# Moving weighted values in TensorE's order of an attention kernel, so that a pair of maxima comes right behind each

## The reference

```
q, k = rope(q), rope(k)
scores = where(causal, q @ k.T / sqrt(16), -inf)
y = softmax(scores) @ v + gating * softmax(q @ ak.T / sqrt(512)) @ av
x = layernorm(x + y @ w_proj.T)
base = x @ base_w.T + base_b;  hidden = x @ A.T;  probs = softmax(x @ router_w.T)
combine = top 2 of probs, divided by their sum
x = layernorm(x + base + 0.5 * sum_e combine[e] * (hidden @ B[e].T))
```

## Time and profile before

| | us |
|---|---|
| median of 3 runs (lowest to highest) | 1001.28 (1001.17 to 1004.49) |
| the profiled execution's own time | 1001.27 |
| its span, first to last instruction | 999.6 |
| PE busy in the span | 900.8 |
| DVE busy | 743.1 |
| ACT busy | 490.0 |
| POOL busy | 240.8 |

### The profile page before, as it was taken

How to read it: one execution, slowest core, us unless ns; L and a number is a source line. 1 busy time by engine, 2 the same in 40 slices (tenths; PEclk the granted TensorE clock), 3 DMA queues, 4 the chain that set the end, 5 groups by cost and what they waited for, 6 DMA issues and landing times. The chain is left out here.

```text
span 999.6 us, 16360 instructions
## 1 busy us (share of the span) xinstructions
PE 900.8 (90%) x5420; PEld 502.0 (50%) x5420; DVE 743.1 (74%) x2254; ACT 490.0 (49%) x1027; POOL 240.8 (24%) x252
## 2 busy tenths in 40 slices
PE   2899999948899999999999999999848999999996
PEld 1778787841222222222223222322237888888884
DVE  3475746569898988889898889896156677777765
ACT  3243334340477777777777777777831211221210
POOL 0215252433121222222222222222202122122211
PEclk9999999985699999999999999999968999999998
DMA  6124242425543335554334545336110010110100
GB/s 216 35 72 116 65 114 74 115 82 128 96 94 58 65 74 96 96 96 81 62 63 84 97 97 96 70 63 158 48 43 11 22 42 21 42 42 21 43 32 31
DMA packets 50401, 74.05 MB, mean 74 GB/s; under 512 B 8864, under 2 KB 21408, under 8 KB 50208
## 3 DMA queue, kind: packets, MB, share of 16 engines
q1 hardware_dynamic: 50336, 73.24, 31.5%
HBM read 56.17 MB, written 16.78 MB: 73 GB/s over the span
## 5 line engine op out<-in xcount | busy, mean ns | idle before, releaser
L720 ACT ACTIVATE pt<-bank 128x512 f32<-128x512 f32 (+3 forms) x768 | 335.2, 493 | 133.2 <-PE bank L1229 122.5
L896 DVE CUSTOM_DVE_ANT_0 bank<-bank,cmask 128x512 f32<-128x512 f32 (+3 forms) x512 | 234.5, 525 | 15.9 <-PE bank L1239 14.1
L1229 PE MATMUL bank<-qs,ks 98*128 98x512 bf16 (+3 forms) x768 | 209.7, 335 | 23.6 <-ACT pt L720 23.3
L578 POOL TENSOR_SCALAR_AFFINE_SELECT pt<-pt 128x512 f32<-128x512 f32 x128 | 81.2, 635 | 368.7 <-ACT pt L720 368.7
L1272 PE MATMUL bank<-pt,vb 128*32 128x512 f32 (+3 forms) x1536 | 164.5, 500 | 0.9 <-POOL pt L578 0.9
L899 DVE TENSOR_REDUCE mx<-bank 128x1 f32<-128x512 f32 x256 | 159.0, 685 | 4.7 <-PE bank L1239 2.6
L1239 PE MATMUL bank<-km,qm 48*128 48x512 bf16 (+3 forms) x768 | 138.9, 347 | 15.7 <-DMA km<-k_parts 11.7
L1229 PEld LDWEIGHTS bank<-qs,ks 98*128 98x128 bf16 x768 | 59.7, 96 | 160.1 <-ACT pt L720 98.2
L1239 PEld LDWEIGHTS bank<-km,qm 48*128 48x128 bf16 x768 | 34.9, 95 | 145.4 <-DVE mx L896 64.0
L745 ACT CAST xth<-bank 128x512 fp32r<-128x512 f32 x16 | 9.4, 585 | 153.8 <-PE bank L1334 153.8
L896 DVE DVE_READ_ACCUMULATOR2_ANT mx<- 128x1 f32 x512 | 73.4, 143 | 0.0
(11 more groups left out here) (141 smaller groups left out, 1378.5 us busy)
## 6 DMA issues: line engine op xcount, KB each, us to landing
qs<-q_parts SPq DMA_DIRECT2D x32, 256.0 KB, 4.7
q_parts<-part SPq DMA_DIRECT2D x48, 128.0 KB, 2.4
k_parts<-part SPq DMA_DIRECT2D x48, 128.0 KB, 2.4
ks<-k_parts SPq DMA_DIRECT2D x16, 384.0 KB, 6.9
xs<-in_xT SPq DMA_DIRECT2D x10, 512.0 KB, 3.6
qm<-q_parts SPq DMA_DIRECT2D x32, 128.0 KB, 7.8
km<-k_parts SPq DMA_DIRECT2D x32, 128.0 KB, 7.3
qs<-q_parts SPq DMA_DIRECT2D x32, 128.0 KB, 3.3
```

Source lines behind the costliest of these rows:

```text
L578: gp.affine_select(out=blk, in_=blk, compare_op=ALU.is_ge, fill=0.0, base=0, pattern=[[0, HG], [1, P]], channel_multiplier=-1).then_inc(S( ...
L720: act.activation(pt[k % PT_BUFS][:, h, 0:width(st)], half(n % SCORE_BUFS)[:, 0:width(st)], ACT.Exp, scale=float(HD) ** -0.5).then_inc(S("e ...
L896: last = ve.tensor_tensor_reduce(blk, blk, cmask[:, BANK - nk * P:], 1.0, NEG, ALU.add, ALU.max, mx[m][:, 0, h, qt:qt + 1])
L1229: pe.matmul(half(n % SCORE_BUFS)[:, 0:q1 - q0], ks[g % 2][0:KX, h, kb * P:(kb + 1) * P], qs[g % 2][0:KX, h, q0:q1], start=True, stop=True) ...
```

## The change

The places of the weighted values are found together with those of the slots: a place must be a score that has two or more slots right behind it, ahead of the next score, and each step takes the first such place at or after the one of `value_place`. As the transposes' places depend on those of the last steps, the two are worked out in turn, five times.

```diff
-VALUES_AT = [value_place(st) for st in range(NS)]
...
+def place_values(first):
+
+    follow = [c for c in range(SCORE_BANKS) if first[(c + 1) % SCORE_BANKS + 1] - first[(c + 1) % SCORE_BANKS] >= 2]
+    at = []
+    for st in range(NS):
+        n = max(value_place(st), at[-1] + 1 if at else 0)
+        if st == LAST_STEP[0] + 1:
+            n = max(n, at[-1] + SCORE_BUFS)
+        while n % SCORE_BANKS not in follow:
+            n += 1
+        at.append(n)
+    while at[-1] - SCORE_BANKS + SCORE_BUFS > at[0]:
+        at[0] += 1
+        while at[0] not in follow:
+            at[0] += 1
+    return at
+
+
+NORM_CHUNK = [9, 25]
+for _ in range(5):
+    VALUES_AT = place_values(place_slots(NORM_CHUNK)[0])
+    COPY_AT = [VALUES_AT[st] for st in LAST_STEP]
+    NORM_CHUNK = [COPY_AT[1] - SCORE_BANKS + 5, COPY_AT[0] + 5]
...
+FIRST, NORM_AT, ROWS_AT = place_slots(NORM_CHUNK)
```

More of the change, by code:

```diff
@@ L100, in value_place, with place_slots @@
     return n
-VALUES_AT = [value_place(st) for st in range(NS)]
[L104 to L108, removed]
 SLOTS = NMX + 3
-NORM_CHUNK = [COPY_AT[1] - SCORE_BANKS + 5, COPY_AT[0] + 5]
 NORM_OF = [(-1, 1), (0, 0)]
-def place_slots():
+def place_slots(norm_chunk):
     read = [sum(nk * P + READ_START for _, _, nk in max_of((LEAD + n) % NMX)[2]) for n in range(NMX)]
@@ L126, in place_slots @@
         first.append(slot)
-        if c in NORM_CHUNK:
+        if c in norm_chunk:
             norm_at.append(slot)
@@ L137, in place_slots @@
     return first + [SLOTS], norm_at, rows_at
-FIRST, NORM_AT, ROWS_AT = place_slots()
+def place_values(first):
[18 more added lines that the diff above has]
+    NORM_CHUNK = [COPY_AT[1] - SCORE_BANKS + 5, COPY_AT[0] + 5]
+assert VALUES_AT == sorted(set(VALUES_AT)) and COPY_AT[0] < SCORE_BANKS <= COPY_AT[1]
+FIRST, NORM_AT, ROWS_AT = place_slots(NORM_CHUNK)
 CALC_AT = ROWS_AT - ROWS_LAG
```

## The result

Over 20 executions each, the changed kernel takes 1006.85 us in the median (1002.39 to 1010.39) and the kernel before 1002.27 (1000.77 to 1007.65); the ratio is 1.0037 with a 95% interval of 1.0019 to 1.0055. So the change makes the kernel slower by about 0.4%, inside the 0.5% that was called no change. Against the range of 993 to 1006.5: the 1001.28 us that the forecast starts from, times the ratio, is 1005.0, inside, while the median of the 20 by itself lies 0.35 above its upper end. The profiled execution took 1002.41 us, 1.14 more than the profiled one of before. The median moved by 4.6. Both numbers need an explanation. One execution of the kernel before, beside e1 to e4, took 1055.56 us at a mean clock of 0.825 and is in no comparison.

What follows compares the result with a forecast made beforehand. TensorE's order of work, with its switches and waits on ScalarE, was taken to bound attention; span 999.6 - 1.0 + 0.5 + 1.4 = 1000.5, plus 1.7 gives 1002.2 us, range 993 to 1006.5.

Steps and rivals of the forecast that it cites:

- Switches: TensorE in each attention head group: six changes of kind fewer at 0.095 us, saving 0.57 us a group.
- Waits that take their place: TensorE's scores waiting on ScalarE: 2.37 us instead of 1.86, +0.51 a group; period 29.32, -1.0 us over 14 groups.
- The last group: Attention's last head group, without maxima and bound by ScalarE: no switch saved, between 0 and +1, taken as +0.5 us.
- The first group: Attention's first head group, partly at half clock: full clock rises later behind a later first block; 0 to +3, taken +1.4 us.
- so no correction: Starting time: the profiled run's 1001.27 us taken as typical, since the three runs' median is 1001.28.
- A: Attention groups: saved switches arrive whole and ScalarE's waits do not grow, -0.57 x 14 = -8.0, 993.8 us; chance 0.15.
- B: Attention groups: the copy's stall returns whole, 0.82 at scores 11 and 27, +1.40 a group, 1022.8 us; chance 0.08.
- C: Attention groups: both stalls shrink and nothing replaces them, -2.04 a group to 27.35, about 973 us; chance 0.06.

Runs made afterwards that it cites:

- e1: The changed kernel once more, unaltered, beside the kernel before: 1004.79 us, ratio 1.0019.
- e4: A third order of weighted values, pairs of maxima and transposes, written out, against the kernel before: 965.57 us, ratio 0.9632, period 26.74 us.
- e2: Half of the change: only four blocks of weighted values that end no half moved, against the kernel before: 1005.97 us, ratio 1.0050, period 29.48 us.
- e3: The other half: only blocks that end a half moved, with ScalarE's copies and transposes, against the kernel before: 1003.67 us, ratio 1.0019, period 29.41 us.
- e7: The kernel before with added products that keep TensorE at work ahead of group 0, against the kernel before: 1001.44 us, ratio 0.9984.
- e8: The changed kernel with the same added products ahead of group 0 as e7, against the kernel before: 1001.67 us, ratio 0.9982.
- e6: The kernel before with two pairs of maxima moved into the two stalls behind ScalarE's copies: 992.15 us, ratio 0.9889, period 28.63 us.
- e5: The kernel before with pairs of maxima moved to the blocks; blocks, copies and transposes stay: 981.53 us, ratio 0.9777, period 27.95 us.
- e9: The order of e4 with the added products ahead of group 0, against the kernel before: 967.61 us, ratio 0.9658, period 26.74 us.
- e10: Another written-out order of values, pairs and transposes, with the added products, against the kernel before: 972.06 us, ratio 0.9701, period 27.15 us.

## Why the prediction was right, and where not

**Switches.** Right: 6 x 0.095 = 0.57. In the profile after, a block holds TensorE 1.00 us ahead of a pair as ahead of a score, and the count fell by six, from 55 to 49. The Trainium skill, TensorEngine Tiling (Array Packing), Key Properties, says that changing the tiling mode drains TensorE, while another tile of the same mode does not; the rows agree: scores and transposes, both on the whole array, follow each other at no cost, and a change from scores to pairs, from pairs to scores or from scores to strips of 32 columns costs 0.09 to 0.10. What leaving the strips costs can't be read apart, as nothing but a change ever follows a block.

**Waits that take their place.** Right to 0.04 us: 19.20 was walked for the stretch from the pair of 0 to that of 33, 19.24 measured, with the late starts at the scores named (6, 23, 32) and in the sizes given (0.42, 0.47, 0.37 for 0.42, 0.46, 0.38). VectorE's idle time of 1.22 before the first normalisation is gone, and the one ahead of the pair of score 9, foreseen as 0.8, is 0.76:

```profile
500.05 0.70 DVE L916 CUSTOM_DVE_ANT_0 bank<-bank,cmask 128x512 f32<-128x512 f32 x1 [0.76 <-PE bank L1259]
```

The period came out at 29.35 for 29.32; over 14 groups -0.55 for -1.0.

**The last group.** +0.73 for +0.5, inside its bounds. ScalarE idles 1.02 and 0.65 us ahead of the two copies there, against 0.37 and none before, more than the 0.3 more that was walked.

**The first group.** +1.35 for +1.4 in the profiled execution, but the reason given did not hold. The term was built on the rise following the first block of weighted values. The rise did come 3.3 us later in the changed kernel, as walked, yet in e2 and e4 that block starts earlier than before and the rise comes 8 us later, and in e3 the block starts 0.7 later and the rise 2.8. So the good fit of this term is in part luck, and what sets the rise is open.

The term was also mis-sized as a property of the kernel: I bounded it at +3 and took the profiled execution for the typical one ("so no correction"). The moment of the rise varies. The median is 4.6 above that of before in the executions of the result, where the profiles differ by 1.1, and 2.4 above in those of e1; single executions lie up to 8 above the fastest. e7 and e8 take the stretch away, and the difference of the medians falls to 0.23. Why the changed order has more long executions than the one before is not shown. A later first block is not enough as a reason: in e2 it stands behind score 11, as before, and three of its ten executions took over 1009. The kernel before had shown the spread: one of its three times was 1004.49, 3 us above the others, and I did not ask why.

**The rivals.** A (switches arrive whole): refuted by the period, and by e2, which saved four and lost. The Trainium skill, Perfetto Trace Analysis, Identifying Performance Opportunities, says that a kernel generally improves by improving its most-contended engine. Here the traces show that this says little of where to save: TensorE was the busiest throughout (28.03 of 29.39 us), 0.57 us less for its switches gave 0.04 a group, and e6 gave 0.76 with no work less. The advice of the Trainium skill, Perfetto Trace Analysis, Optimization Strategy, to find the gaps of that engine and what blocks it there is what e5, e6 and e4 follow. B (stall returns whole) did not occur: scores 11 and 27 start 0.10 late or less. C was not to be had by this change; e4, another order, shows that a period below C's 27.35 exists.

## What to carry to other kernels

Where two engines hand each other work through few buffers, first list the stalls of the busier one by the score, tile or step they stand ahead of; then move independent work into them, and only then count what the neighbours cost (0.76 us a group for two moved pairs in e6, against 0.04 for six saved switches in the change). A rule for the neighbours alone (here: a pair behind every block) moves the very blocks and copies that made or covered a stall. Periodic stages can be walked from start-to-start times: six orders came out within 0.2 us of 27 to 29, and one, in which VectorE holds TensorE, 0.6 too low; the ends of a stage, where the clock rises or other engines fall idle, need their own terms and several executions.

## What the runs showed of the hardware

- Being busy did not bring the full clock: in e2 TensorE was busy 16.46 of 16.60 us at 0.50 of 2.4 GHz, with the first block of weighted values in it. With the added products group 0 ran at 1.00 throughout in e7 and e8; in e9 and e10 it fell to 0.50 for 3.4 and 3.3 us, in e9 with TensorE busy 3.40 of 3.40 us. Whether the products' kind or their amount does it was not tried.
- The time of one program on one core took several levels, up to 8 us apart, which go with the mean of the granted clock: from 1002.4 us at 0.953 to 1010.1 at 0.946 in the changed kernel, by estimate half a microsecond for each at half clock.
